# Causal attention with one exponential over two PSUM banks: eight banks divided anew

## What is computed

```python
x = x + attn(layernorm(x))
    # qkv = h @ Wqkv + bqkv; softmax(q k^T / 8, causal) v; then @ Wproj + bproj
x = x + ffn(layernorm(x))
    # h @ W.T + b + (h @ V_r) @ C.T
```

## Time and profile before

| | us |
|---|---|
| median of 3 runs | 895.28 (892.41 to 899.08) |
| profiled execution, its own time | 894.46 |
| its span on core 7 | 892.9 |
| spans of the eight cores | 881.6 to 892.9 |
| DVE busy / ACT busy / POOL busy on core 7 | 281.1 / 352.8 / 185.7 |
| mean granted TensorE clock, share of full | 0.864 |

### The profile page before, as it was taken

One profiled execution on the slowest core, in us unless ns is written; L12 is line 12 of the kernel. 1 busy time (PEld: TensorE's weight loads), 2 busy tenths in 40 slices (PEclk: granted clock), 3 DMA queues, 4 the chain that ended last, 5 costly groups with the idle time before them and its releaser, 6 DMA issues.

```text
span 892.9 us, 11448 instructions; the slowest of 8 cores (881.6 to 892.9 us)
## 1 busy us (share of the span) xinstructions
PE 704.1 (79%) x3433; PEld 297.9 (33%) x3433; DVE 281.1 (31%) x675; ACT 352.8 (40%) x769; POOL 185.7 (21%) x304
## 2 busy tenths in 40 slices
PE   0499999997168888888888897888897988667656
PEld 0244444443133333333333333333232333222222
DVE  2443433202025422334232333312132231432342
ACT  0141413140025554634655657565657566300000
POOL 2000000001025332433222323222202222311311
PEclk9999999999555557789899999989899989878698
DMA  8990200001920000011010100101010000111001
GB/s 169 217 194 19 74 22 24 1 1 27 173 82 1 1 1 25 1 47 41 8 48 1 48 34 15 48 1 49 0 48 1 25 25 1 47 48 47 25 24 47
DMA packets 15131, 38.18 MB, mean 43 GB/s; under 512 B 3401, under 2 KB 3425, under 8 KB 15073
## 3 DMA queue, kind: packets, MB, share of 16 engines
q0 software_dynamic: 7616, 11.67, 8.4%
q1 hardware_dynamic: 7457, 25.79, 7.9%
HBM read 39.68 MB, written 8.39 MB: 54 GB/s over the span
## 4 chain that ended last, share of the span: by engine, by line
PE 71%; DVE 9%; ACT 7%; issue 6%; DMA 4%; POOL 2%; DVEq 0%; SPq 0%; ACTq 0%; POOLq 0%
PE ps_pv L412 15%; PE ps_sp L428 9%; PE ps_w L543 6%; PE ps_sp L255 5%; PE ps_pv L255 5%; PE ps_u L428 5%; PE ps_w L612 4%; ACT xnt_a L435 4%; PE ps_pv L612 4%; PE ps_bf L239 4%; PE ps_sp L282 3%; PE ps_w L282 3%; ACT xf_a L435 3%; PE ps_u L255 3%; DMA xf_a<-wffn 2%
## 5 line engine op out<-in xcount | busy, mean ns | idle before, releaser
L435 ACT ACTIVATE xnt_a<-ps_sp 128x512 bf16<-128x512 f32 (+3 forms) x285 | 142.3, 539 | 146.0 <-PE ps_sp L428 109.2
L428 PE MATMUL ps_sp<-q_fm,k_fm 64*128 64x512 bf16 (+3 forms) x427 | 135.7, 394 | 43.1 <-ACT xnt_a L435 28.1
L442 POOL TENSOR_TENSOR xnt_a<-xnt_a,tri_sb 128x128 bf16<-128x128 bf16 x142 | 57.4, 425 | 256.5 <-ACT xnt_a L435 255.4
L412 PE MATMUL ps_pv<-xnt_a,v_on 128*66 128x512 bf16 (+3 forms) x356 | 109.2, 411 | 1.7 <-POOL xnt_a L442 1.3
L428 PE MATMUL ps_u<-q_fm,k_fm 64*128 64x512 bf16 (+2 forms) x213 | 84.7, 398 | 23.2 <-ACT xf_a L435 14.6
L435 ACT ACTIVATE xf_a<-ps_u 128x512 bf16<-128x512 f32 (+3 forms) x142 | 76.3, 537 | 50.7 <-PE ps_sp L428 43.9
L412 PE MATMUL ps_pv<-xf_a,v_on 128*66 128x512 bf16 (+3 forms) x284 | 90.2, 413 | 2.1 <-POOL xf_a L442 1.5
L435 ACT ACTIVATE xf_a<-ps_sp 128x512 bf16<-128x512 f32 (+3 forms) x142 | 70.8, 542 | 47.5 <-PE ps_sp L428 24.9
L442 POOL TENSOR_TENSOR xf_a<-xf_a,tri_sb 128x128 bf16<-128x128 bf16 x114 | 46.2, 425 | 144.7 <-ACT xf_a L435 143.4
L428 PEld LDWEIGHTS ps_sp<-q_fm,k_fm 64*128 64x128 bf16 x427 | 33.2, 95 | 127.3 <-issue 122.8
L481 DVE RECIPROCAL recips<-ps_bf 128x4 f32<-128x4 bf16 x64 | 11.7, 183 | 186.4 <-PE ps_bf L471 183.1
(11 more groups left out here) (77 smaller groups left out, 794.5 us busy)
## 6 DMA issues: line engine op xcount, KB each, us to landing
xf_a<-x SPq DMA_DIRECT2D x32, 512.0 KB, 3.4
y<-xf_a SPq DMA_DIRECT2D x16, 512.0 KB, 2.6
wq_a<-wqkv POOLq DMA_DIRECT2D x3, 2048.0 KB, 38.3
wq_a<-wproj POOLq DMA_DIRECT2D x1, 2048.0 KB, 19.0
xf_a<-wffn POOLq DMA_DIRECT2D x4, 512.0 KB, 25.4
bias_a<-bqkv POOLq DMA_DIRECT2D x1, 512.0 KB, 56.3
bias_a<-bffn POOLq DMA_DIRECT2D x1, 512.0 KB, 59.8
bias_a<-bproj SPq DMA_DIRECT2D x1, 512.0 KB, 8.6
```

The lines of the kernel that those rows point to most:

```text
L412: e.matmul(ps_pv[hd][0:66, off * 128:512], v_on[:, ki2, 66 * hh:66 * hh + 66], chunk(cb)[:, 0:ncol], start=st, stop=sp),
L428: e.matmul(sbanks[sb][:, off * 128:512], k_fm[hp:hp + 64, hc, ki * 128:(ki + 1) * 128], q_fm[hp:hp + 64, hc, g * 512 + off * 128:(g + 1) * ...
L435: e.activation(chunk(cb)[:, 0:ncol], sbanks[sb][:, off * 128:512], AF.Exp, bias=0.0, scale=0.125),
L442: gate = P.op("pool", lambda e, cb=cb: e.tensor_tensor(chunk(cb)[:, 0:128], chunk(cb)[:, 0:128], tri01[:], ALU.mult), waits=[m_ex, m_cm], ...
```

## The change

The banks are divided anew, and three things follow from it.

1. Scores: four banks (ps_sc) as two pairs of banks. The scores of both heads of a block go into one pair of banks; the first of the two matmuls waits, for the exponential of two blocks earlier. One ACTIVATE takes the exponential over both banks ([128, 2, ncol]) into a chunk pair; there are four chunk pairs. So there are 320 exponentials where there were 640. The triangle multiplications stay, two for each diagonal block, both behind the one exponential. The order of PVs and fillers stays.
2. ps_w has one bank. The second half of a projection, and of an FFN in stage B, waits for the residual add of the first half; the residual adds are of 512 columns each.
3. The FFN's residual adds in the tail are each emitted behind their own half. In stage A q and k rotate over four banks, and v goes through the two ps_pv banks, half by half.

The core of the diff (the deleted lines of the stage A part and of the FFN's adds left out):

```diff
-        ps_sp = E(nc.psum_tensor("ps_sp", [128, 1024], F32))
-        ps_w = E(nc.psum_tensor("ps_w", [128, 1024], F32))
-        ps_u = E(nc.psum_tensor("ps_u", [128, 512], F32))
+        ps_sc = E(nc.psum_tensor("ps_sc", [128, 2048], F32))
+        ps_w = E(nc.psum_tensor("ps_w", [128, 512], F32))
...
+                for half in range(2):
+                    m_v_evac[half] = P.op("dve", lambda e, kt=kt, half=half: e.tensor_tensor(
+                                        v_on[:, kt, half * 528:(half + 1) * 528]
...
             for ki in range(K):
...
+                pp = gki % 2
+                cp = gki % 4
                 for hd, hp in ((0, 0), (1, 64)):
-                                waits=[sb_reader[sb], m_qkv_done], sig="pe")
-                    m_ex = P.op("act", lambda e, sb=sb, cb=cb, off=off, ncol=ncol:
-                                e.activation(chunk(cb)[:, 0:ncol],
-                                             sbanks[sb][:, off * 128:512], AF.Exp,
+                                waits=[pair_reader[pp], m_qkv_done] if hd == 0 else [],
+                                sig="pe" if hd == 1 else None)
+                m_ex = P.op("act", lambda e, pp=pp, cp=cp, off=off, ncol=ncol:
+                            e.activation(chunkpair(cp).rearrange("p (a n) -> p a n", a=2)
+                                         [:, :, 0:ncol],
+                                         ps_sc[:, pp * 1024:(pp + 1) * 1024]
+                                         .rearrange("p (a n) -> p a n", a=2)
+                                         [:, :, off * 128:512], AF.Exp,
+                                         bias=0.0, scale=0.125),
+                            waits=[m_sc, ch_reader[cp]], sig="ac")
+                pair_reader[pp] = m_ex
...
             for half in range(2):
                 for kc in range(KC):
                     mmp = P.op("pe", lambda e, half=half, kc=kc, aoTv=aoTv:
-                               e.matmul(ps_w[:, half * 512:(half + 1) * 512],
+                               e.matmul(ps_w[:, 0:512],
...
+                               waits=([m_aoT, m_wproj, r_psw] if kc == 0 else [])
+                                     if half == 0 else
+                                     ([m_x2] if kc == 0 else []),
+                               sig="pe")
+                m_x2 = P.op("dve", lambda e, i2=i2, i3=i3, half=half: e.scalar_tensor_tensor(
+                                x2b(i2)[:, half * 512:(half + 1) * 512], ps_w[:, 0:512], 1.0,
+                                x_rr(i3)[:, half * 512:(half + 1) * 512], ALU.mult, ALU.add),
...
-                if half == 0 and not use_pv:
-                    w0.append(r_psw)
+                if not use_pv:
+                    w0.append(r_psw if half == 0 else m_y)
```

More of the change, by code:

```diff
@@ L244, in transpose8 @@
             return m_tr
-        qkv_banks = [ps_s[0], ps_s[1], ps_pv[0], ps_pv[1], ps_u[:, 0:512]]
+        qkv_banks = [ps_sc[:, i * 512:(i + 1) * 512] for i in range(4)]
         def mats_gen(tb):
@@ L275, in mats_gen @@
                 kt = tb * 4 + tt
-                vp = tt % 2
-                vdst = ps_w if vp == 0 else ps_sp
-                mmv = None
+                mmv = [None, None]
                 for half in range(2):
                     for kc in range(KC):
-                        mmv = P.op("pe", lambda e, half=half, kc=kc, tbuf=tbuf, tt=tt, vdst=vdst:
-                                   e.matmul(vdst[:, half * 512:(half + 1) * 512],
+                        mmv[half] = P.op("pe", lambda e, half=half, kc=kc, tbuf=tbuf, tt=tt:
+                                   e.matmul(ps_pv[half][:, 0:512],
                                             xnT(tbuf)[:, kc, tt * 128:(tt + 1) * 128],
@@ L432, in emit_B_pair @@
                                          tile_position=(hp, 0), skip_group_check=True),
[L433 to L439 removed]
+                                waits=[pair_reader[pp], m_qkv_done] if hd == 0 else [],
[9 more added lines that the diff above has]
+                pair_reader[pp] = m_ex
+                for hd in range(2):
                     gate = m_ex
                     if ki >= 4 * g:
[L442 to L443 removed]
+                        gate = P.op("pool", lambda e, cp=cp, hd=hd: e.tensor_tensor(
+                                        chunkpair(cp)[:, hd * 512:hd * 512 + 128],
+                                        chunkpair(cp)[:, hd * 512:hd * 512 + 128],
                                         tri01[:], ALU.mult),
                                     waits=[m_ex, m_cm], sig="pl")
[L446 to L447 removed]
+                    pend.append((cp, off, ncol, gate, ki, hd))
+                gki += 1
                 if ki % 2 == 1:
@@ L546, in gen_C1a2 @@
                                         start=(kc == 0), stop=(kc == KC - 1)),
-                               waits=[m_aoT, m_wproj, r_psw] if (half == 0 and kc == 0) else [],
-                               sig="pe" if (half == 1 and kc == KC - 1) else None)
+                               waits=([m_aoT, m_wproj, r_psw] if kc == 0 else [])
[5 more added lines that the diff above has]
+                                x_rr(i3)[:, half * 512:(half + 1) * 512], ALU.mult, ALU.add),
+                            waits=[mmp, m_xpb] + ([r_x2[i2]] if half == 0 else []), sig="dv")
                 yield
             r_aoT[i2] = mmp
-            m_x2 = P.op("dve", lambda e, i2=i2, i3=i3: e.scalar_tensor_tensor(
-                            x2b(i2), ps_w[:], 1.0, x_rr(i3), ALU.mult, ALU.add),
-                        waits=[mmp, m_xpb, r_x2[i2]], sig="dv")
             r_psw = m_x2
@@ L599, in fdst @@
             def fdst(half):
-                return ps_pv[half][:, 0:512] if use_pv else \
-                    ps_w[:, half * 512:(half + 1) * 512]
+                return ps_pv[half][:, 0:512] if use_pv else ps_w[:, 0:512]
             mmf = None
+            m_y = None
             for half in range(2):
                 w0 = [m_hT, m_wt_evac]
-                if half == 0 and not use_pv:
-                    w0.append(r_psw)
+                if not use_pv:
+                    w0.append(r_psw if half == 0 else m_y)
                 if use_pv:
@@ L623, in gen_C2 @@
                            sig="pe")
+                m_y = P.op("dve", lambda e, i2=i2, half=half, mmf=mmf: e.scalar_tensor_tensor(
+                               x2b(i2)[:, half * 512:(half + 1) * 512],
+                               fdst(half), 1.0,
+                               x2b(i2)[:, half * 512:(half + 1) * 512],
+                               ALU.mult, ALU.add),
+                           waits=[mmf, m_x2f] if half == 0 else [mmf], sig="dv")
+                if use_pv:
+                    r_pvffn[half] = m_y
                 yield
             r_hT[i2] = mmf
-            if use_pv:
-                m_y = None
-                for half in range(2):
-                    m_y = P.op("dve", lambda e, i2=i2, half=half: e.scalar_tensor_tensor(
-                                   x2b(i2)[:, half * 512:(half + 1) * 512],
-                                   ps_pv[half][:, 0:512], 1.0,
-                                   x2b(i2)[:, half * 512:(half + 1) * 512],
-                                   ALU.mult, ALU.add),
-                               waits=[mmf, m_x2f] if half == 0 else [mmf], sig="dv")
-                    r_pvffn[half] = m_y
-            else:
-                m_y = P.op("dve", lambda e, i2=i2: e.scalar_tensor_tensor(
-                               x2b(i2), ps_w[:], 1.0, x2b(i2), ALU.mult, ALU.add),
-                           waits=[mmf, m_x2f], sig="dv")
+            if not use_pv:
                 r_psw = m_y
```

87 lines of the change are left out of this document (36 added, 51 removed).

## The result

The changed kernel takes 876.77 us (median) against 896.66 for the one before; the ratio is 0.978 (95% interval 0.9762 to 0.9799), 19.7 us faster. The prediction was 872, with 855 to 894. In the two profiled executions the slowest core goes from 892.9 (core 7) to 874.9 us (core 1), and the mean span of the eight cores from 888.6 to 868.5.

A forecast was written before the change was run, and what follows sets the result against it. No engine is full, PE leads (704 of 893 us); latencies limit light cycles, POOL the diagonals, PE heavy pairs. Terms -15.7 - 11.1 - 5.8 - 3.0 - 1.5 + 14.3 + 0.2 = -22.6 from 894.46 give 871.9, said as 872, range 855 to 894.

The forecast's parts named there:

- The exponential: On ACT, a merged exponential of 1024 columns takes 1.03 us, pitch 0.92; merging saves only 0.06 us per block.
- Light cycles: Two-block cycles, mostly in light pairs of g=2 and g=3, fall from 2.51 to 1.95 us: 28 x 0.56 = 15.7 us gained.
- Pair starts: First four blocks of pairs in g=1 to 3: fifth exponential at 4.35 us instead of 4.95, gaining 11.1 us in all.
- more than forecast: Rival, chance 0.1: denser PE work removes low-clock stretches at pair starts and ps_w's waits cost only 0.5 us, giving 855.
- Diagonal blocks: In diagonal blocks POOL limits next: first exponential to last PV 4.42 us instead of 4.60, gaining 5.8 us over 32 pairs.
- The single ps_w bank: In stage B's FFNs and projections, second halves wait for the first's add: 19 x 0.75 = 14.3 us lost, 3.0 regained.
- Stage A: The q, k and v stage: a wait of 1.48 us goes and no new one comes, so -1.5 us.
- Tail: After attention: five projections lengthen the layernorm chain by 3.2 us, split FFN adds give -3.0, net +0.2 us.
- the clock takes the gain: Rival, chance 0.2: PE's clock drops behind pair starts, costing 19 us and giving 891, the same as before within 1%.
- The one bank costs more: Rival, chance 0.1: second halves behind 24 ps_w waits run at low clock, costing 41 us in all, giving 913.
- The merged exponential doesn't merge well: Rival without its own chance: crossing the bank costs the fixed part again, pitch 0.98 and length 1.2, giving 882.

The follow-up runs named there:

- e2_exp_each: The changed kernel with one exponential per bank (640 of them), each triangle multiplication behind its own exponential: 871.62 us, ratio 0.9716.
- e5_no_tri: The changed kernel without the triangle multiplications, so masking inside the diagonal squares is left out: 823.93 us, ratio 0.9173.
- e10_mask_pe: The changed kernel with the diagonal mask added by PE matmuls before the exponential and no multiplication after it: 827.95 us, ratio 0.9226.
- e1_one_w: The kernel before with only one ps_w bank and the halved residual adds, scores and exponentials as before: 903.31 us, ratio 1.0072.
- e12_tail_sc: The changed kernel with the tail's five projections going into the first two banks of ps_sc: 866.42 us, ratio 0.9667.
- e3_phase: The changed kernel with one more empty filler step at the start of the FFN generator: 875.53 us, ratio 0.976.
- e4_tri_split: The changed kernel with the second head's triangle multiplication on DVE instead of POOL: 856.60 us, ratio 0.9559.

## Why the prediction was right

The direction, and the size within 5 us: 872 foretold, 877 measured. The steps for the fourth bank, for POOL and for the single ps_w bank hold; that the sum came so near is in part luck, since one term of 11 us is nearly absent and others that were not foreseen made up for it. By its steps:

- *The exponential*: 1.03 us foretold, 1.023 measured; ACT is busy for 329 us, near 334 was foretold. That merging itself gives little stood in the prediction; e2_exp_each shows it.
- *Light cycles*: 1.95 foretold, 1.91 measured, 28 of them. Right where the clock is full. The first cycle of each light pair gained nothing, for the clock; the 24 cycles of the light pairs gave 10.9 us instead of 13.4.
- *Pair starts*: 11.1 us foretold, 3.0 measured (from a pair's first scores to its fifth exponential, summed over the 24 pairs of g=1 to 3, mean of the cores: light ones 5.5 shorter, heavy ones 2.5 longer). This is the term that was mis-sized. Its chain to 4.35 us lets the second exponential follow the first at once and puts nothing on PE before the fourth scores; with the layernorm's activations or a filler's transposes there it is 4.88 to 4.98 even at full clock, and the 4.95 of before was right. On top, the clock falls there. So light pairs of g=3 gained 2.0 us each instead of 3.0, and heavy ones of g=2 lost 1.7 instead of 0.7.
- *The clock in g=1*: in no term of the sum. It rose from 0.73 to 0.89 and g=1 gained 8.1 us instead of 3.7. Every kernel with four score banks shows it (2 to 29 us at the lower level in g=1, 43 to 50 in the three kernels with three banks), so it comes with the change, but by no step of mine; it is the mechanism of *more than forecast*, at another place.
- *Diagonal blocks*: 4.42 foretold and measured in light pairs and in g=3; POOL as the limit is shown by e5_no_tri and e10_mask_pe. The heavy pairs of g=2 had half of a projection there and lost 0.95 each. Not seen was the second price of the stall: with less of it, the clock behind it stays up.
- *The single ps_w bank*: 19 waits of 0.75 foretold, 19 with 14.4 us measured; net of the 3.0 that go, e1_one_w gives 11.2 us in stage B where 11.3 was foretold. This term was right.
- *Stage A*: -1.5 foretold for the one wait, which is gone; -4.3 measured. The three kernels with the old stage A read 260.9 to 262.6, those with the new one 257.6 to 259.8: some 3 us are real, half of them unexplained.
- *Tail*: +0.2 foretold, +0.9 measured, but e12_tail_sc finds 6 to 7 us at the single bank, of which my 3.2 is the part that a shorter add doesn't make up.

Of the rivals, *the clock takes the gain* was real as a mechanism: 54 us at the lower level in g=2 and g=3 became 73. (Before, 13 of their 16 pairs had such a stretch, not ten.) Its net over B is small beside the 19 of that case: light pairs of g=3 fell short by 4.0 us and heavy ones of g=2 by 4.0, g=1 gave 4.4 more. I had set it up as an alternative; it is a part of every case. *The one bank costs more* fell with e1_one_w. *The merged exponential doesn't merge well* fell by its row of 1023 ns.

## What to carry to other kernels

Price a freed wait by what is late next (here POOL, eight multiplications in a row), and take away that one before or together with it: the same bank change was worth 20 us with it and 52 without. When a chain is priced at a new place, list everything that stands in both queues there: two activations of 0.2 and 0.3 us took away most of a gain of 0.6 us per pair. Before a wait of an engine whose clock depends on its work is called cheap, look at the granted clock behind it: filling a microsecond of waiting with useless matmuls gave 35 us, and the same matmuls behind a gap cost 58. A PSUM bank shared by two halves costs the round trip over the evacuating engine for every pair of halves without other work between them; moving the halves by one step (e3_phase) moved the wait.

## What the runs showed of the hardware

- Two score matmuls on rows 0 to 63 and 64 to 127 of the array, released together, take 0.39 us together in the trace (720.12), as one alone (0.38 at 736.00 before).
- An exponential over two PSUM banks takes 1023 ns for 1024 columns against 602 for 512, and starts 0.91 to 0.92 behind the one before it.
- The granted clock: in the changed kernel 73 of 351 us of g=2 and g=3 are at the lower level, behind pairs' ends that wait for POOL and starts where PE waits 1.0 us twice for an exponential; with the six extra matmuls in the start 6.5 of 325, and without POOL's multiplications 18 (mean of the cores). 192 matmuls that compute nothing made the kernel 35 us faster.
- POOL and DVE beside each other: a 128x128 bf16 multiplication on POOL takes 425 ns in the mean when POOL does all of them, and 465 and 519 (by buffer) when DVE does every second one (e4_tri_split); on DVE it takes 223 and 312.
